# Selective scan on one Trainium2 core: TensorE's order within a unit, twelve slots for the products with C, and repeated B and C loaded in quarters

## What is computed

```
def step(h, inp):
    x_t, d_t, B_t, C_t = inp
    dA = jnp.exp(d_t[:, :, None] * A)
    h = dA * h + (d_t * x_t)[:, :, None] * B_t[:, None, :]
    y = jnp.einsum('bdn,bn->bd', h, C_t) + D_param * x_t
    return (h, y)
...
out = x_path * jax.nn.silu(z_path)
```

## Time and profile before

| what | value |
|---|---|
| median of 3 runs | 4515.22 us (4509.1 to 4519.24) |
| profiled execution | 4513.32 us |
| its span in the trace | 4511.6 us |
| busy over the span | DVE 77%, PE 76%, ACT 43%, POOL 36% |
| first transfer of the scan stage issued | 3012.24 us |
| first recurrence starts | 3041.6 us |
| first and last product with C start | 3060.9 and 3931.6 us |
| one product with C on POOL, one scan on DVE | 2.35 us, 2.28 to 2.34 us |

### The profile page before, as it was taken

One profiled execution on the slowest core, in us unless ns is written; L12 is line 12 of the kernel. 1 busy time (PEld: TensorE's weight loads), 2 busy tenths in 40 slices (PEclk: granted clock), 3 DMA queues, 4 the chain that ended last, 5 costly groups with the idle time before them and its releaser, 6 DMA issues. The chain is left out here.

```text
span 4511.6 us, 58933 instructions
## 1 busy us (share of the span) xinstructions
PE 3415.4 (76%) x16218; PEld 1440.9 (32%) x16219; DVE 3484.3 (77%) x4984; ACT 1934.9 (43%) x2362; POOL 1624.8 (36%) x920
## 2 busy tenths in 40 slices
PE   4859999999999999538977377626667667647665
PEld 1513333233323332325654233201111111136554
DVE  5758888888888886463436969947889888779998
ACT  0506666666666667200011155523444444323232
POOL 0110000000000000370016415548889988835454
PEclk7959999999999999759986688857777777778887
DMA  1630101011010100422222324241111111121110
GB/s 53 236 102 3 40 4 41 9 35 40 4 41 5 39 3 5 152 89 76 64 75 88 107 83 148 103 141 54 57 57 63 61 57 58 55 71 37 43 37 15
DMA packets 234106, 276.42 MB, mean 61 GB/s; under 512 B 41944, under 2 KB 189280, under 8 KB 232544
## 3 DMA queue, kind: packets, MB, share of 16 engines
q1 hardware_dynamic: 217264, 243.35, 17.4%
q0 software_dynamic: 6144, 16.79, 1.2%
q10 hardware_dynamic: 10544, 14.22, 0.9%
HBM read 153.83 MB, written 120.08 MB: 61 GB/s over the span
## 5 line engine op out<-in xcount | busy, mean ns | idle before, releaser
L866 DVE TENSOR_REDUCE att_maxima<-att_ps_m 128x1 f32<-128x512 f32 x2048 | 1280.5, 682 | 261.5 <-PE att_ps_m L909 257.9
L840 ACT ACTIVATE att_probs<-att_ps_s 128x1024 f32<-128x1024 f32 x1024 | 996.3, 1021 | 444.2 <-PE att_ps_s L923 441.6
L909 PE MATMUL att_ps_m<-att_ks,att_qs 96*128 (+1 forms) x2048 | 730.8, 393 | 46.6 <-DMA att_ks<-scratch_k 28.5
L923 PE MATMUL att_ps_s<-att_qs,att_ks 99*128 (+1 forms) x2048 | 612.9, 381 | 24.4 <-DMA att_qs<-att_m_parts 22.2
L2167 POOL TENSOR_TENSOR ss_ch<-ss_h,ss_c_rep 128x1024 f32<-128x1024 f32 x256 | 594.8, 2351 | 1.8 <-DVE ss_h L2213 1.6
L931 PE MATMUL att_ps_o<-att_probs,att_vs 128*32 128x512 f32 x4096 | 547.2, 606 | 0.4 <-ACT att_probs L840 0.4
L2188 ACT ACTIVATE ss_ps_d<-ss_ps_d,ss_a_neg 128x1024 f32<-128x1024 f32 x256 | 278.6, 1088 | 516.8 <-PE ss_ps_d L2253 516.6
L909 PEld LDWEIGHTS att_ps_m<-att_ks,att_qs 96*128 (+1 forms) x2048 | 165.3, 97 | 640.9 <-DVE att_maxima L866 367.0
L2275 PE MATMUL ss_ps_y<-ss_ch,ss_sum_block 128*32 128x256 f32 x2048 | 220.8, 517 | 148.5 <-POOL ss_ch L2167 148.5
L2245 PE MATMUL ss_ps_x<-ss_stack,ss_spread 96*128 96x512 bf16 x512 | 205.5, 492 | 146.9 <-ACT ss_skip L2176 75.4
L2213 DVE TENSOR_TENSOR_SCAN ss_h<-ss_ps_d,ss_u 128x1024 f32<-128x1024 f32 x128 | 289.1, 2276 | 30.4 <-ACT ss_ps_d L2188 15.9
(11 more groups left out here) (413 smaller groups left out, 5297.7 us busy)
## 6 DMA issues: line engine op xcount, KB each, us to landing
scratch_steps<-si_parts SPq DMA_DIRECT2D x48, 512.0 KB, 5.8
ss_stack<-scratch_steps SPq DMA_DIRECT2D x256, 96.0 KB
att_qs<-scratch_q SPq DMA_DIRECT2D x192, 64.0 KB
ex_x<-scratch_sorted_x SPq DMA_DIRECT2D x72, 128.0 KB
scratch_sorted_y<-ex_y SPq DMA_DIRECT2D x72, 128.0 KB
scratch_v<-qkv_v_ext SPq DMA_DIRECT2D x8, 1024.0 KB, 4.4
att_vs<-scratch_v SPq DMA_DIRECT2D x8, 1024.0 KB
moe_w_w<-in_W ACTq DMA_DIRECT2D x16, 512.0 KB, 12.1
```

Source lines behind the costliest of these rows:

```text
L840: act.activation(probs[:, (2 * kt + pair) % 4, :, :], ps_s[pair][:, :, :], ACT.Exp, scale=HD ** -0.5).then_inc(exp_done, 1)
L866: dve.tensor_reduce(maxima[:, j, c:c + 1], ps_m[BANK[j * QC + c]][:, :], AX.X, ALU.max).then_inc(maxed, 1)
L909: pe.matmul(ps_m[BANK[j * QC + c]][:, :], q, k, start=True, stop=True).then_inc(scored, 1)
L923: mm = pe.matmul(ps_s[pair][:, i, :], ks[0:ROWS, bass.ds(st // QC % 2, 1), h, kt * P:(kt + 1) * P], qs[0:ROWS, bass.ds(st // QC % 2, 1), b ...
```

## The change

There are four edits, all in `selective_scan`:

1. On TensorE a unit is now `spread_x`, `spread_d`, the D term, then the chunk of sums. Chunks stand one unit later: the first of a group at n mod 4 = 3, where it waits for the product with C of unit n-4. The D term moves from place 6 to place 7, the last chunk of a part to place 6 of the next, and VectorE's gate with it.
2. `ch` has 12 slots, three groups, so GpSimd waits for the sums of three groups back.
3. `b_rep` and `c_rep` are loaded in four quarters each of 1024 columns (512 KB), in turn B, C, B, C, by ScalarE's queue at the start of the stage. Who reads a quarter waits for that quarter.
4. SP's loads of `zs` and stores of `gated` move from place 9 to place 11 of a part.

```diff
-        ch = r.sb("ch", [P, 2 * JQ, HALF])
+        ch = r.sb("ch", [P, CH_GROUPS * JQ, HALF])
...
-        SUMS_FROM, SUMS_TO = JQ + 2, GROUPS_HERE + JQ + 1
+        SUMS_FROM, SUMS_TO = JQ + 3, GROUPS_HERE + JQ + 2
...
-                load_rep(b_rep, 0, "loaded")
...
-                    if w.n == STACKS - 1:
-                        load_rep(c_rep, 1, "c_loaded")
...
-                    if w.i == JQ + 5:
+                    if w.i == JQ + 7:
...
-                pool.wait_ge(s["c_loaded"], 16)
-                pool.wait_ge(s["loaded"], 3 * 16)
...
+                    pool.wait_ge(b_loaded[w.cols.start // HALF], 16)
...
-                    if w.n >= 2 * JQ:
-                        pool.wait_ge(s["y_steps"], w.n // JQ - 1)
-                    pool.tensor_tensor(ch[:, w.n % (2 * JQ), :], h[:, w.i, :], c_rep[:, w.cols], ALU.mult).then_inc(s["ch_ready"], 1)
+                    if w.dt == 0 and w.i == 0:
+                        pool.wait_ge(c_loaded[w.cols.start // HALF], 16)
+                    if w.n >= CH_GROUPS * JQ:
+                        pool.wait_ge(s["y_steps"], w.n // JQ - CH_GROUPS + 1)
+                    pool.tensor_tensor(ch[:, w.n % (CH_GROUPS * JQ), :], h[:, w.i, :], c_rep[:, w.cols], ALU.mult).then_inc(s["ch_ready"], 1)
...
-                act.wait_ge(s["loaded"], 3 * 16)
+                for c in range(T // HALF):
+                    for i, (dst, loaded) in enumerate(((b_rep, b_loaded), (c_rep, c_loaded))):
+                        act.dma_start(dst[:, c * HALF:(c + 1) * HALF],
+                                      over(scratch.bc[i * NS:(i + 1) * NS, c * HALF:(c + 1) * HALF].unsqueeze(0), [DG, NS, HALF])).then_inc(loaded[c], 16)
+                act.wait_ge(s["loaded"], 2 * 16)
...
-                dve.wait_ge(s["loaded"], 3 * 16)
...
+                    if w.dt == 0 and w.i < 2:
+                        dve.wait_ge(b_loaded[w.cols.start // HALF], 16)
...
-                    group, q = (n // JQ - 1, n % JQ - 2) if n % JQ >= 2 else (n // JQ - 2, n % JQ + 2)
+                    group, q = (n // JQ - 1, 0) if n % JQ == JQ - 1 else (n // JQ - 2, n % JQ + 1)
...
                     spread_x(w)
+                    spread_d(w)
                     if w.i == SUMS_FROM:
                         skip_term(w)
                     sums_at(w.n)
-                    spread_d(w)
```

More of the change, by code:

```diff
@@ L2064, in selective_scan @@
         ps_d, ps_x, ps_y = r.ps("ps_d", [P, 2, HALF]), r.ps("ps_x", [P, HALF]), r.ps("ps_y", [P, HALF])
-        names = ("loaded", "c_loaded", "padded", "tables", "a_exp", "skip_ready", "d_ready", "x_ready", "decay_ready", "u_ready", "x_copied",
+        names = ("loaded", "padded", "tables", "a_exp", "skip_ready", "d_ready", "x_ready", "decay_ready", "u_ready", "x_copied",
                  "pool_u_ready", "h_ready", "ch_ready", "skipped", "y_steps", "gated_ready")
@@ L2069, in selective_scan @@
         stack_loaded = [r.sem(f"stack_loaded{i}") for i in range(STACKS)]
+        b_loaded, c_loaded = ([r.sem(f"{n}{c}") for c in range(T // HALF)] for n in ("b_loaded", "c_loaded"))
         xc_loaded, zs_loaded, gated_stored = r.sem("xc_loaded"), [r.sem(f"zs_loaded{i}") for i in range(2)], [r.sem(f"gated_stored{i}") for i in range(2)]
@@ L2080, in _ @@
                 sp.dma_start(d_col[:, :], io["D_param"]).then_inc(s["loaded"], 16)
-                def load_rep(dst, i, loaded):
-                    sp.dma_start(dst[:, :], over(scratch.bc[i * NS:(i + 1) * NS, :].unsqueeze(0), [DG, NS, T])).then_inc(s[loaded], 16)
-                load_rep(b_rep, 0, "loaded")
                 sp.wait_ge(s["padded"], 2)
@@ L2274, in sums @@
                     for jq in range(JQ):
-                        mm = pe.matmul(ps_y[jq * 32:(jq + 1) * 32, cols], block[:, jj, :], ch[:, (jj % 2) * JQ + jq, cols],
+                        mm = pe.matmul(ps_y[jq * 32:(jq + 1) * 32, cols], block[:, jj, :], ch[:, (part * JJ + jj) % CH_GROUPS * JQ + jq, cols],
                                        start=False, stop=jj == JJ - 1 and q % 2 == 1)
@@ L2290, in _ @@
                     sums_at(w.n)
-                    spread_d(w)
-                for n in range(SCAN_UNITS, SCAN_UNITS + JQ + 2):
+                for n in range(SCAN_UNITS, SCAN_UNITS + JQ + 3):
                     sums_at(n)
+CH_GROUPS = 3
 TABLES = 1 + 2 * PARTS + 1 + 1 + JJ + 2 * JJ
```

## The result

The changed kernel takes 4533.34 us (median of 7 runs, 4524.59 to 4540.64), the kernel before, on the same chips, 4518.96 us (7 runs, 4509.10 to 4525.65). The ratio is **1.0034, 95% interval 1.0020 to 1.0047**: slower by 0.34%, some 15 us, where 4465 and a gain of 50 were forecast.

The account below looks back on a forecast made before the run. The prediction took the scan stage to be bound by a ring of waits between GpSimd and TensorE. 4513.3 less 30 (steps and turns) and 20 (start) gave 4463 for the profiled execution, 4465 as median; range 4425 to 4500.

Parts of the forecast that it names:

- a ring from GpSimd's product by way of TensorE back to GpSimd: Scan stage: GpSimd waits for itself, its next input's spread_x queued behind sums of its product; about 1 us in ten.
- GpSimd's floor of 3.077 us a unit: Scan stage: GpSimd without a wait takes 9.23 us for three products and one input, against 10.24 taken.
- Within a part: New order and later chunks: 3.1 us a unit taken, ends 3.077 and 3.2, where 3.415 was measured before.
- the level will still swing: TensorE's clock level within parts: swings, with TensorE at work about 60% of the time; GpSimd's lag hides most low stretches.
- At the turn: Old part's last chunk and D term behind spread_d: GpSimd idles 3.1 us a turn, ends 1.3 and 3.9, sixteen times.
- Twelve slots: GpSimd's product waits for sums of three groups back: that wait never ends last; brings nothing itself.
- The quarters: Stage start, tables loaded in quarters: 20 us saved, the middle between 8 and 31.
- the 8: Stage start: us saved if every stack load must let a whole quarter pass; rival "loads queue", 4477, chance 0.20.
- The rival for the other side, that the low level takes over: Scan stage: clock stays at 1.2 GHz, three units take 9.6 us, turns about 5.9 more; 4535, slower, chance 0.07.
- the point of no gain: Scan stage: slower once the low level holds for about three fourths; start's 20 used up at 891 us.
- the three signs of being wrong: Profile after: VectorE's spread_x wait as large as before; stack loads holding TensorE after 3060; clock well under 0.75.
- The tail: Stage's end, last product to last gate: the same four chunks as before, at no change.

Follow-up runs that it names:

- e3: Changed kernel with the old order within a unit (spread_x, D term, chunk of sums, then spread_d): ratio 0.9791 to the kernel before.
- e8: e3 with each half of the D term ahead of the chunk that first needs it (places 7 and 8): ratio 0.9777 to the kernel before.
- e9: e8 with six of the eight quarters issued later, singly: 4409.18 us, ratio 0.9761 to the kernel before.
- e11: e9 with two zero products between chunk of sums and spread_d in every place but 6 and 7: ratio 0.9771 to the kernel before.
- e10: Changed kernel with three zero products behind each spread_x but place 7's: ratio 0.9910 to the kernel before, 56 us under the changed kernel.
- e5: Changed kernel with the old order within a unit in places 6 and 7 of each part alone: ratio 0.9928 to the kernel before.
- e12: Kernel before with loads in quarters and 12 slots for products with C, TensorE's order and chunks' places as before: ratio 0.9956.
- e1: Kernel before with the table loads in quarters alone: ratio 0.9960 to the kernel before.
- e7: e3 with spread_d ahead of the D term in place 7: ratio 0.9867 to the kernel before.

## Why the prediction was wrong

The reading of before was right: a ring from GpSimd's product by way of TensorE back to GpSimd, 1 us in 10 with nobody working for it, and GpSimd's floor of 3.077 us a unit, which e3, e8, e9 and e11 come within 2% of. What failed are sizes in two steps, and the choice between cases.

**Within a part** I worked out 3.077 at the high level and 3.2 at the low, with `spread_x` 0.8 us late, and took 3.1. The mechanism is there to the tenth (0.87 us of VectorE's idle), but with 1.9 us of idle in a part's 12 places outside the turn the pace is 3.077 + 1.9 / 12 = 3.24, at and a little past the low level's end. The step that failed is "the level will still swing": the granted clock fell from 0.75 to 0.62. e10 shows that the level is all of the cost within a part: at 0.95 the idle there is some 0.1 us. Why the level fell is shown in part. e3, with the wait gone and the old order, holds 0.71, so most of the fall comes with the new order within a unit. What in that order lowers it is open; that the long wait had been followed by dense stretches, and that the low level feeds itself by way of the late spread, are guesses that no run tests.

**At the turn** the step took 3.1 us, from ends of 1.3 and 3.9. It measured 5.9 (6.8, 6.4 and 4.5): 1.8 at place 5, which was charged nothing, and 4.1 at places 6 to 8. Two things were wrong. First, I let GpSimd be 2.3 us behind VectorE when the gate stalls, and so charged nothing to its product at place 5. For units with n mod 3 = 2 in places 0 to 3 and 10 to 15 the product starts 1.1 us behind the scan's end in the changed kernel (1.9 in e3, 1.8 in e10), so the reserve is gone before the gate's 2 us are over, and GpSimd waits for `h`. The mean over all units hides this: it is 2.3 us in the changed kernel too. That the smaller reserve is the cause fits the runs with it (place 5 idles 2.0, 3.2 and 0.3 us in the changed kernel, and 0.2, 1.2 and 0 in e10), but no run sets it alone. So the turn and the places ahead of it don't add up singly: with the turn's order mended alone (e5, reserve 1.1) its places still idle 2.1 us on average, and 1.1 in e3 (reserve 1.9). Second, I took the D term between the levels; in 10 of 16 parts of the changed kernel it takes the full 3.62 us, and in none under 2.9. The row that said so was in my hands, low after 1.73 us of idle, and I had worked out idles of 2.5 and 1.4.

In time: the turn was 2.8 us off at 15 turns (not 16: the first part's D term waits for no gate), some 40 us, and the pace 0.14 at 12 places of 16 parts, some 25. The two make about the 61 us by which the steps missed: 901.3 us (906.9 less 5.6 of the start's, see below) for 840.

**Twelve slots** bring nothing by themselves: right (e12). **The quarters** save 20 at the start, from ends of 8 and 31: right, 19.4 at unit 6 and 18 in the ratio of e1. ScalarE's eight issues were to end 5.7 us after the stage's start and ended after 11.8, and two stack loads held TensorE up; both lie between the ends. The middle was taken because no row spoke for either end, so that it came out so near is in part luck. As for the rule of the Trainium skill, "DMA: Bandwidth & Descriptors", section "Queues, rings and completion order", beside which I set the 8: it speaks of a whole packet of descriptors, and that a `stack` load must let a whole quarter pass was a step of mine. The spreads of units 4 and 5 stand 6.0 us apart (3034.73 and 3040.71), the very pace of that step, but `xc`, 1 MB, went ahead of unit 5's rows too, and the spreads of units 3 and 4 stand 4.7 and those of 5 and 6 stand 2.2 us apart (3030.05 and 3042.95). So the step did not set the sum, and the runs do not settle the rule. e9 shows the mechanism: with six quarters out of the way both waits are gone.

**The choice.** The rival for the other side, that the low level takes over, named the right mechanism and the right sign, and its steps were near: 3.2 us a unit (3.24 measured outside the turns) and 5.9 a turn (5.9), 910 us from first to last product (906.9, of which 5.6 are the `stack` loads' at the start), 4535 in all (4533). That the totals meet so closely is luck in part: it had the low level throughout, and put the point of no gain at about three fourths of the stage; the level was low for three quarters, and the kernel was 15 us slower. I gave it 0.07. Its price was worked out with the same care as the forecast's; its chance was not. What spoke for it, TensorE at work 60% of the time and idles growing ahead of the D term, stood in my own text.

**Signs to look for.** TensorE's idle for the products under 20: right (5.5). First product with C near 3035 to 3045: 3031.6 by the clock of an execution whose stage began 4.3 us earlier, so at the early edge. New idle of VectorE ahead of gates: right, 2.2 rather than 1.2. Four D-term products of 1.06 us: right. GpSimd's wait for the copy under 55: wrong (108). Of the three signs of being wrong two came: a clock "well under 0.75" (0.62), and a VectorE wait for `spread_x` as large as before (101.8, for 87.3). The third did not: the `stack` loads held TensorE up at 3034.73 and 3040.71 and not after 3060. The tail was to stay as it was; VectorE's wait for its last gate went from 6.6 to 7.4 us.

What stays open: what in the new order lowers the clock, and how much of the turn's 4.2 us in e10 is the D term's clock and how much its place. A version with the new order and a high clock at place 7 was not tried, since at place 7, between the gate and the D term, `ps_y` holds no open sum to add zeros to.

## What to carry to other kernels

When a wait is moved to where its event has long come, move the wait alone. What else stands between a long chain's result and the next link (here a chunk of sums and the D term, behind the product that waits for the scan) is on the chain from then on. Price the chain at both levels of TensorE's clock, and give the low level its chance: both the wait that was taken away (0.75 to 0.71) and the new order of the same work (0.71 to 0.62) lowered the clock here. And an engine that lags absorbs a stall only as far as its lag at that very unit goes; read it there, not as a mean.

## What the runs showed of the hardware

Work that computes nothing made a kernel faster: 699 zero products, 189 us of TensorE's time, took the granted clock of the stretch from 0.62 to 0.95 and the kernel 56 us down (e10 against the changed kernel). On the kernel with the good order, where GpSimd idled 0.5 us a part, 434 of them took the clock of the same stretch from 0.71 to 0.92 and gained no time that can be told (e11 against e9).

The clock follows the order of the same work: 0.71 with each unit's `spread_d` behind the chunk of sums (e3), 0.62 with it ahead (the changed kernel), though TensorE waits little for the products in either (19.2 and 5.5 us).

Of eight transfers of 512 KB issued in a row on ScalarE's queue, the first took 1.22 us to issue, five about 0.6, the seventh 1.39 and the eighth 5.91, and ScalarE's first activation waited behind it (the changed kernel; in e1, e3, e7, e10 and e12 the eighth took 5.8 to 6.0). With two issued, the second took 0.62 (e9).
